# Local attention of a four-layer block: scores in 64-row halves, values three tiles behind, the next norm in its drain

## The chip, the cores and the metric

The kernel runs on one core of a Trainium2 chip. The metric is the device time of one launch in microseconds (us), the median of the runs shown. Engines are named as the profile names them: PE is the matrix engine (PEld its weight loads), DVE the vector engine, ACT the scalar engine, POOL the general-purpose engine, SP the engine that only issues DMAs. Each runs its own instructions strictly in order and waits on semaphores.

## The reference

Sixteen sequences of 1024 tokens with 256 features pass through four residual layers, each behind a layer norm without weights:

```
x = x + local_attention(layernorm(x), w_qkv, b_qkv)
x = x + ffn(layernorm(x), cn_*, gc_*, adaptive_range)
x = x + differential_attention(layernorm(x), Wq, Wk, Wv, Wo, ...)
x = x + ffn(layernorm(x), cn_*, gc_*, adaptive_range)
```

Local attention has 16 heads of 16 features. Every 32 neighbouring tokens form a group of their own, and attention is computed inside a group: `softmax(q k^T / 4) v` with 32x32 scores. Its output is reshaped without moving the heads back beside the features, so one "token" of the output holds one head's values of 16 tokens. The feed-forward layer (ffn) runs three cycles of a small gelu network (256 to 256 to 128 to 64 to 1) that sets one coupling factor per token, `out = out + coupling * twist(out)`, and adds to the factor a global one from the mean over all tokens of a sequence (`global_net`). Everything here is in float32, which PE works through in two passes: each float32 matmul stands in the trace as two records.

## The kernel before, in words

The 16 sequences are taken in 8 pairs, one turn of a hardware loop per pair. A turn is a chain of blocks, and each block ends when all engines have ended it: `local_attention`, `layernorm("n2")`, `ffn("f1")`, `layernorm("n3")`, `diff_attention`, `diff_output`, `layernorm("n4")`, `ffn("f2")`. The order of the instructions of each engine is written out by hand in each block.

**`local_attention`** takes a pair as 16 tiles of 128 tokens, t = 0 to 15, eight per sequence; a tile has four groups of 32 tokens. For each tile, with the line numbers of the kernel before:

- POOL copies the keys into `kx`, once for each head, with all rows but those of that head set to zero (L444). One instruction makes the 8 heads of one half c of the features: 8 times 128 columns. There are 4 buffers, so POOL can be two tiles ahead.
- PE, `scores` (L376): for each half c and each group k one matmul of 128 rows, weights the 32 queries of the group, moving 8 heads times 32 masked keys, to the 32 PSUM partitions of the group. The four groups stand in four column strips of the array. The scores of a tile fill one PSUM bank, and two banks alternate by t % 2, so a tile's scores wait for the `shift` of two tiles before.
- DVE: `maximum` (L469), `shift` (L473, subtracts the maximum and so frees the bank), and of the tile before `total` (L478), `inverse` (L482), and `turn` (L486 the division, L490 a transpose in 32x32 blocks).
- ACT: `exponentials` (L540), `keep` (L553, the values of tile t - 3 to `hT`) and `place` (L548, four copies that set the turned weights of tile t - 1 into a matrix with zeros around the groups). There are two such matrices.
- PE, `values` (L392): 16 matmuls, of tile t - 2 behind the scores of tile t.

Between these, PE projects the second sequence: four query and key pieces (L352) at t = 2 to 5 and four value pieces (L361) at t = 6 to 9 (and the first sequence's value pieces at t = 0 and 1), which ACT and DVE take out of PSUM (L534, L460). From t = 11 PE turns the first sequence's output into the reshaped order (`regroup`, L410), and DVE adds it to x (`residual`, L497) and takes the statistics for the next norm (L503). The second sequence's four `regroup` pieces come after the last tile, when nothing else is left.

**`layernorm("n2")`** then finishes the statistics of the second sequence (L244, L246, POOL's root L252), normalises 16 tiles of tokens on DVE (L271), turns them on PE (L258) and copies them back to SBUF as `hT` (ACT L304, DVE L277).

**`ffn("f1")`** begins with the mean over each sequence (DVE L1009) and its first layer: `layer1(n)` for chunk n of 512 tokens is four pieces of two matmuls each, two with `w1` and two with `w1t` (L697). The first matmuls of layer 2 are at L706; the global network is at L678 to L686.

Of the kernel before, what the change touches and what calls it, by code (L numbers as in the profile page):

```python
# [51 lines left out]
def build(nc, a, out, scratch, rows):  # L52
    B = a["x"].shape[0]
    PAIRS = B // PB
    with ExitStack() as ctx:
# [44 lines left out]
        hmask = sb("hmask", [P, LC])  # L100
# [152 lines left out]

        def norm_turned(pe, t, s_h, s_tp):
# [7 lines left out]
        def layernorm(tag, norm, ahead=None, stale=None):  # L262
# [3 lines left out]
            with nc.Block() as block:  # L266
                @block.vector
                def _(v):
                    def normalised(n):
                        for t in range(4 * n, 4 * n + 4):  # L270
                            v.tensor_scalar(h[:, t, :], x[:, t, :], mv[:, t, 0:1], rstd[:, t:t + 1],  # L271
                                            ALU.subtract, ALU.mult).then_inc(s_h, 1)

# [8 lines left out]
                    for n in range(N0, CH + 1):  # L282
                        if n < CH:
                            if n % NB == 0:
                                v.wait_ge(norm[2], n // NB + 1)
                            normalised(n)
# [20 lines left out]
        def local_attention(norm):  # L307
# [8 lines left out]
            kx = [hh[:, i * N:(i + 1) * N].rearrange("p (h n) -> p h n", h=LC) for i in range(4)]  # L316
# [23 lines left out]
            with nc.Block() as block:  # L340
                @block.tensor
                def _(pe):
# [23 lines left out]
                    def scores(t):  # L366
# [3 lines left out]
                        if t >= 2:  # L370
                            pe.wait_ge(s_sd, t - 1)
                        for c in range(C):
                            pe.wait_ge(s_kx, C * t + c + 1)
                            for k in range(BLK):
                                r = slice(k * LB, (k + 1) * LB)
                                mm = pe.matmul(ps[r, t % 2, c * 256:(c + 1) * 256],  # L376
                                               qkT[:, b, c, tb * P + k * LB:tb * P + (k + 1) * LB],
                                               kx[(C * t + c) % len(kx)][:, :, r],
                                               start=True, stop=True)
                            mm.then_inc(s_sc, 1)  # L380

                    def values(t):
# [1439 lines left out]
```

## Time and profile before

| | us |
|---|---|
| Median of 3 runs | 7971.05 (7957.34 to 7980.41) |
| The profiled execution, its own time | 7964.95 |
| Its span, first to last instruction | 7963.3 |

The profile puts PE at 7373.2 us busy (93% of the span), DVE at 6889.1 (87%), ACT at 6124.5 (77%) and POOL at 3628.6 (46%). Most of that is `diff_attention`. These are means over blocks with different limits; the blocks that the change touches are a small part of each turn and are read by themselves below. PE's clock has two levels, 1.2 and 2.4 GHz, and the granted clock is given as a share of the upper one: 0.963 over the span.

### The profile page before, as it was taken

To read this page: it belongs to the slowest core of one execution; us is meant where nothing else is said; L and a number is where in the kernel's file an instruction comes from. 1 tells how busy PE (TensorE), PEld (TensorE's weight loads), DVE (VectorE), ACT (ScalarE), POOL (GpSimd) and SP (SyncE) were. 2 spreads that over 40 slices of the span, in tenths; PEclk is the share of its full clock that TensorE was granted. 3 is DMA by queue.
4 is the path that set the end of the run, shared out by engine and by line. 5 is a ranking of instruction groups with operands and counts; after the bars stand their busy time and mean duration, and the time that the engine had idled before them with its cause. 6 is when DMAs were issued, how large, how long until landed. Compare 5 with 4: busy or idle time off the path is not lost. (4 is left out here: it accounts for less than half of the span.)

```text
span 7963.3 us, 182322 instructions
## 1 busy us (share of the span) xinstructions
PE 7373.2 (93%) x72640; PEld 3328.7 (42%) x72640; DVE 6889.1 (87%) x8962; ACT 6124.5 (77%) x11390; POOL 3628.6 (46%) x5187
## 2 busy tenths in 40 slices
PE   6899988999889998899988999889998999989999
PEld 4344443444434444344443444434444344443444
DVE  5899868997689976899769997699976999769997
ACT  3699756997569975699756997569975699756997
POOL 4366333663336623466234662346613466135661
PEclk9999999999999998999989999999999999999999
DMA  1122102120022100222002220021200222002210
GB/s 32 53 45 44 30 12 56 44 48 24 12 56 48 44 24 12 57 48 44 23 12 59 47 45 24 10 64 44 47 23 5 64 44 48 26 2 64 48 44 26
DMA packets 604400, 298.88 MB, mean 38 GB/s; under 512 B 487094, under 2 KB 528566, under 8 KB 603510
## 3 DMA queue, kind: packets, MB, share of 16 engines
q1 hardware_dynamic: 603516, 286.86, 14.8%
q8 instruction: 583, 9.55, 0.5%
q14 instruction: 301, 2.47, 0.1%
HBM read 123.84 MB, written 67.37 MB: 24 GB/s over the span
## 5 line engine op out<-in xcount | busy, mean ns | idle before, releaser
L1548 DVE TENSOR_REDUCE mall<-ps 128x1 f32<-128x1024 f32 x4096 | 4669.5, 1217 | 71.7 <-PE ps L1482 68.4
L1639 ACT ACTIVATE work<-ps 128x512 f32<-128x512 f32 x8192 | 4311.2, 603 | 164.0 <-PE ps L1498 39.9
L1514 PE MATMUL ps<-work,vbuf 128*32 128x256 f32 x32768 | 2624.3, 392 | 21.6
L1498 PE MATMUL ps<-qop,kop 51*128 51x256 bf16 x16384 | 2558.1, 273 | 10.6 <-ACT work L1639 8.8
L1482 PE MATMUL ps<-kop,qop 48*128 48x512 bf16 x8192 | 2535.4, 384 | 33.6 <-DMA kop<-scratch 18.8
L1498 PEld LDWEIGHTS ps<-qop,kop 51*128 51x128 bf16 x16384 | 1182.0, 94 | 1887.5 <-ACT work L1639 1596.1
L1514 PEld LDWEIGHTS ps<-work,vbuf 128*32 128x32 f32 x32768 | 661.8, 108 | 923.4 <-issue 591.1
L252 POOL TENSOR_TENSOR rstd<-rstd,nhalf 128x8 f32<-128x8 f32 x64 | 109.3, 1707 | 1501.9 <-DVE rstd L246 1501.9
L1573 POOL TENSOR_TENSOR mall<-mall 128x8 f32<-128x8 f32 x1024 | 212.9, 208 | 1254.9 <-DVE mall L1548 1214.8
L444 POOL TENSOR_TENSOR hh<-work,hmask 128x1024 f32<-128x1024 f32 x256 | 516.2, 2045 | 457.0 <-POOLq L1744 362.1
L1601 POOL TENSOR_TENSOR work<-work,none 128x16 f32<-128x16 f32 x224 | 650.4, 2904 | 18.1
L1482 PEld LDWEIGHTS ps<-kop,qop 48*128 48x128 bf16 x8192 | 538.5, 93 | 93.6 <-DVE mall L1548 58.7
L706 PE MATMUL ps<-work,w 128*128 128x512 f32 x768 | 401.4, 663 | 62.9 <-ACT work L843 62.9
L1598 POOL COPY work<-work 128x272 uint16<-128x272 uint16 x448 | 221.7, 495 | 478.5 <-DMA work<-work 464.4
L548 ACT COPY vbuf<-qop 32x512 f32<-32x512 f32 x512 | 315.2, 616 | 105.6 <-DVE qop L490 96.0
L1614 POOL TENSOR_TENSOR work<-work,nhalf 128x8 f32<-128x8 f32 x224 | 373.2, 1666 | 18.6
L258 PE MATMUL ps<-ident,hh 128*128 128x128 f32 x800 | 167.6, 390 | 161.6 <-DVE hh L271 83.2
L304 ACT COPY hh<-ps 128x512 f32<-128x512 f32 x80 | 46.9, 586 | 325.5 <-PE ps L258 325.5
L392 PE MATMUL ps<-vbuf,work 128*32 128x128 f32 x4096 | 159.7, 304 | 143.4 <-ACT vbuf L548 141.9
L1582 POOL COPY work<-hh 128x512 uint16<-128x512 uint16 x448 | 260.6, 611 | 42.5 <-ACT hh L1646 28.9
L706 PEld LDWEIGHTS ps<-work,w 128*128 128x128 f32 x768 | 153.6, 211 | 285.7 <-issue 165.9
L1646 ACT COPY hh<-ps 128x256 f32<-128x256 f32 x512 | 190.5, 372 | 90.7 <-PE ps L1514 90.7
(179 smaller groups left out, 8317.1 us busy)
## 6 DMA issues: line engine op xcount, KB each, us to landing
qop<-scratch SPq DMA_DIRECT2D x512, 64.0 KB
scratch<-work SPq DMA_DIRECT2D x32, 768.0 KB, 4.3
scratch<-hh SPq DMA_DIRECT2D x32, 768.0 KB, 3.8
kop<-scratch SPq DMA_DIRECT2D x256, 96.0 KB
vbuf<-in_x SPq DMA_DIRECT2D x9, 2048.0 KB, 8.4
qop<-scratch SPq DMA_DIRECT2D x512, 32.0 KB
kop<-scratch SPq DMA_DIRECT2D x256, 64.0 KB
qop<-mT SPq DMA_DIRECT2D x1024, 3.0 KB
```

Source lines behind the costliest of these rows:

```text
L444: pool.tensor_tensor(kx[i % len(kx)], qkT[:, b, 2 + c, tb * P:(tb + 1) * P][:, None, :].to_broadcast([P, LC, P]), hmask[:, :, None].to_bro ...
L548: act.copy(PT[t % 2][r, :, r], pr[t % 2][r]).then_inc(s_pa, 1)
L706: mm = pe.matmul(ps[:, 2 * n, :], w2[:, c, :], a1[n][:, c, :], start=c == 0, stop=c == C - 1)
L1482: pe.matmul(ps[:, b + n, :], qop[r:r + KQ, s, i, t * P:(t + 1) * P], kop[r:r + KQ, s, i, half(n)], start=True, stop=True).then_inc(s_ms, 1)
L1498: mm = pe.matmul(ps[:, bank, part * HQ:(part + 1) * HQ], kop[r:r + KM, s, i, (t + part) * P:(t + part + 1) * P], qop[r:r + KM, s, i, quart ...
L1514: mm = pe.matmul(ps[VW * i:VW * (i + 1), OB, kept], vp[:, b, t, (G * gl + i) // 2, :], prob[:, u % PS, i, cols], start=t == 0, stop=t == T ...
L1548: v.tensor_reduce(mall[:, m // CUT % 2, to, col:col + 1], ps[:, b:b + NB, :].rearrange("p b n -> p (b n)"), AX.X, ALU.max).then_inc(s_mr, 1)
L1582: pool.tensor_copy(plane16[u], src[:, :, u]).then_inc(s_pl, 1)
L1598: link(pool.tensor_copy(raw_halves[:, :, :, u], turned16[u].rearrange("p t (h w) -> p (t h) w", w=VW)[:, :, 0:LD + 1]))
L1601: link(pool.tensor_tensor(erz, y[:, :, LD], none[:, :], ALU.pow))
L1614: link(pool.tensor_tensor(err, esv, nhalf[:, 0:HV], ALU.pow))
L1639: act.activation(prob[:, u % PS, hl, :], ps[:, EB[slot % len(EB)], :], ACT.Exp, scale=scale).then_inc(s_ex, 1)
```

## The change

- **Scores.** The rows of a half c are cut in two: s = 0 is rows 0 to 63, the first four heads, s = 1 rows 64 to 127, the other four. The mask `hmask` has four columns instead of eight, so one POOL instruction writes 4 times 128 columns, in which each row half holds its own four heads. There are 8 buffers of half the size. A tile's scores are 16 matmuls of 64 rows and 128 moving columns instead of 8 of 128 rows and 256. Half s goes to bank s, so a tile uses both banks at once and its scores wait for the `shift` of the tile just before. DVE's `maximum` and `shift` read 256 columns of each of the two banks; the heads stand in another order, which `placed_at` undoes in `values`.
- **Values.** `values` runs three tiles behind the scores, not two.
- **The norm.** The block `layernorm("n2")` is gone. In `local_attention` DVE normalises the first sequence right behind the last `turn`, PE turns it (`first_turns`) ahead of the last `values`, and ACT and DVE copy it. In `ffn("f1")` PE does three of the four pieces of the first chunk, then turns the second sequence, then goes on; DVE's statistics, normalising and copies of the second sequence stand around the first mean.
- **Both ffn blocks.** The first step of the global network stands behind both `w1` pieces of chunk 1, not between them.
- A helper is renamed (`scaled`), and `normalised` becomes shared by the blocks.

```diff
-        hmask = sb("hmask", [P, LC])
+        hmask = sb("hmask", [P, LC // 2])
+        def normalised(v, n, s_h):
+            for t in range(4 * n, 4 * n + 4):
+                v.tensor_scalar(h[:, t, :], x[:, t, :], mv[:, t, 0:1], rstd[:, t:t + 1],
+                                ALU.subtract, ALU.mult).then_inc(s_h, 1)
...
-            kx = [hh[:, i * N:(i + 1) * N].rearrange("p (h n) -> p h n", h=LC) for i in range(4)]
+            kx = [hh[:, half(i)].rearrange("p (h n) -> p h n", h=LC // 2) for i in range(8)]
...
-                        if t >= 2:
-                            pe.wait_ge(s_sd, t - 1)
+                        if t >= 1:
+                            pe.wait_ge(s_sd, t)
                         for c in range(C):
                             pe.wait_ge(s_kx, C * t + c + 1)
-                            for k in range(BLK):
-                                r = slice(k * LB, (k + 1) * LB)
-                                mm = pe.matmul(ps[r, t % 2, c * 256:(c + 1) * 256],
-                                               qkT[:, b, c, tb * P + k * LB:tb * P + (k + 1) * LB],
-                                               kx[(C * t + c) % len(kx)][:, :, r],
-                                               start=True, stop=True)
+                            for s in range(2):
+                                heads = slice(s * P // 2, (s + 1) * P // 2)
+                                for k in range(BLK):
+                                    r = slice(k * LB, (k + 1) * LB)
+                                    mm = pe.matmul(ps[r, s, c * P:(c + 1) * P],
+                                                   qkT[heads, b, c, tb * P + k * LB:tb * P + (k + 1) * LB],
+                                                   kx[(C * t + c) % len(kx)][heads, :, r],
+                                                   start=True, stop=True)
                             mm.then_inc(s_sc, 1)
...
-                                                   vz[:, b, tb, i, :], PT[t % 2][:, i, :], start=e == 0, stop=e == 1,
+                                                   vz[:, b, tb, i, :], PT[t % 2][:, placed_at(i), :], start=e == 0, stop=e == 1,
...
+                    def first_turns():
+                        for t in range(T):
+                            pe.wait_ge(s_h, t + 1)
+                            for c, bank in enumerate((t // 4, VB + 2 + t // 4)):
+                                mm = pe.transpose(ps[:, bank, t % 4 * P:(t % 4 + 1) * P],
+                                                  h[:, t, c * P:(c + 1) * P], ident[:, :])
+                            mm.then_inc(s_tp, 1)
...
+                            if k >= 2:
+                                pe.wait_ge(s_ld, k - 1)
...
-                    for t in range(TT + 2):
+                    for t in range(TT + 3):
                         if t < TT:
                             scores(t)
-                        if t >= 2:
-                            values(t - 2)
+                        if t == TT + 3 - 1:
+                            first_turns()
+                        if t >= 3:
+                            values(t - 3)
...
-                        v.tensor_reduce(mx[:, t, :], scores_of(t), AX.X, ALU.max).then_inc(s_mx, 1)
+                        v.tensor_reduce(mx[:, t, :].rearrange("p (s h) -> p s h", s=2), scores_now, AX.X,
+                                        ALU.max).then_inc(s_mx, 1)
...
+                    v.wait_ge(norm[2], 1)
+                    for n in range(NB):
+                        normalised(v, n, s_h)
+                    for n in range(NB):
+                        v.wait_ge(s_tp, 4 * (n + 1))
+                        v.tensor_copy(hT[:, 0, 1, half(n)], ps[:, VB + 2 + n, :]).then_inc(s_ld, 1)
                     for k in range(4):
                         residual(1, k)
...
-                    layer1(0)
-                    layer1(1, ((0, 0),))
+                    if second_norm:
+                        layer1(0, ((0, 0), (0, 1), (1, 0)))
+                        for t in range(T, TT):
+                            norm_turned(pe, t, s_h0, s_tp0)
+                        layer1(0, ((1, 1),))
+                        pe.wait_ge(s_lc, CH)
+                        pe.wait_ge(s_ld, CH)
+                    else:
+                        layer1(0)
+                    layer1(1, ((0, 0), (0, 1)))
                     global_net(0)
-                    layer1(1, ((0, 1),))
...
-                    for b in range(PB):
+                    if second_norm:
+                        spread(v, norm0, 1)
+                    mean(0)
+                    if second_norm:
+                        v.wait_ge(norm0[2], 2)
+                        for n in range(NB, CH):
+                            normalised(v, n, s_h0)
+                        for n in range(NB, CH):
+                            second_keep(n)
+                    mean(1)
                     keep(0)
...
-            layernorm("n2", n2)
```

PE's order at t = 2 and 3 of `local_attention`, as a difference (L376 and L378 are the scores before and now, L392 and L399 the values, L352 the projection pieces; out and in are the buffers):

```order
-L376 MATMUL ps<-hh,work 32x256 x8
-L392 MATMUL ps<-vbuf,work 32x128 x16
+L378 MATMUL ps<-hh,work 32x128 x16
 L352 MATMUL ps<-hh,w_qkv 128x512 x4
-L376 MATMUL ps<-hh,work 32x256 x8
-L392 MATMUL ps<-vbuf,work 32x128 x16
+L378 MATMUL ps<-hh,work 32x128 x16
+L399 MATMUL ps<-vbuf,work 32x128 x16
 L352 MATMUL ps<-hh,w_qkv 128x512 x4
```

The first `values` have moved behind the scores of t = 3, and the scores are twice as many matmuls with half the columns.

PE's order from the last scores to the global network, before (L410 is `regroup`, L258 the norm's transposes, L697 the first layer of the ffn, L678 the global network's first step):

```order
L376 MATMUL ps<-hh,work 32x256 x8
L392 MATMUL ps<-vbuf,work 32x128 x48
L410 MATMUL ps<-ident,hh 64x64 x64
L340 UNCONDITIONAL_BRANCH
L294 UNCONDITIONAL_BRANCH
L258 MATMUL ps<-ident,hh 128x128 x32
L266 UNCONDITIONAL_BRANCH
L671 UNCONDITIONAL_BRANCH
L697 MATMUL ps<-hh,w 128x512 x4
L697 MATMUL ps<-hh,w1t 128x512 x4
L697 MATMUL ps<-hh,w 128x512 x2
L678 MATMUL ps<-work,g 128x2 x2
```

and the same place now (L408 are the `first_turns`, L263 the second sequence's transposes, L427 `regroup`, L732 the first layer, L713 the global network):

```order
L399 MATMUL ps<-vbuf,work 32x128 x48
L408 MATMUL ps<-ident,hh 128x128 x16
L399 MATMUL ps<-vbuf,work 32x128 x16
L427 MATMUL ps<-ident,hh 64x64 x64
L340 UNCONDITIONAL_BRANCH
L706 UNCONDITIONAL_BRANCH
L732 MATMUL ps<-hh,w 128x512 x4
L732 MATMUL ps<-hh,w1t 128x512 x2
L263 MATMUL ps<-ident,hh 128x128 x16
L732 MATMUL ps<-hh,w1t 128x512 x2
L732 MATMUL ps<-hh,w 128x512 x4
L713 MATMUL ps<-work,g 128x2 x2
```

One block with 32 transposes is gone; 16 of them stand ahead of the last tile's values, and 16 behind six matmuls of the first layer.

## Rows read from the trace of the kernel before

**Rows 1.** Windows of pairs 2 and 3: length, busy PE, PEld, DVE, ACT, POOL, clock.

```profile
1113.00:1137.00 24.00, 18.83 (x384) 13.94 (x376) 20.52 (x41) 16.44 (x31) 16.76 (x8) 1.00 0.01 2
2096.00:2123.00 27.00, 20.58 (x384) 15.30 (x376) 22.66 (x42) 16.32 (x30) 15.86 (x8) 0.87 0.01 2
```

**Rows 2.** Timeline, pair 2, tiles 8 to 10: start, us, engine, line, count, idle before.

```profile
1103.17 1.07 PE L376 MATMUL ps<-hh,work 128*32 128x256 f32 x16
1104.31 0.69 DVE L469 TENSOR_REDUCE work<-ps 128x16 f32<-128x512 f32 x1 [1.18 <-PE ps L376]
...
1107.15 2.54 ACT L548 COPY vbuf<-qop 32x512 f32<-32x512 f32 x4 [0.50 <-DVE qop L490]
...
1108.47 0.69 DVE L469 TENSOR_REDUCE work<-ps 128x16 f32<-128x512 f32 x1
...
1109.74 1.08 PE L392 MATMUL ps<-vbuf,work 128*32 128x128 f32 x32 [1.34 <-ACT vbuf L548]
...
1111.20 0.85 DVE L460 TENSOR_TENSOR work<-ps,b_v 128x128 f32<-128x128 f32 x4
...
1112.67 1.07 PE L376 MATMUL ps<-hh,work 128*32 128x256 f32 x16
```

**Rows 3.** Timeline of PE, pair 2, tiles 2, 3 and 6.

```profile
1069.85 1.07 PE L376 MATMUL ps<-hh,work 128*32 128x256 f32 x16
1072.14 1.08 PE L392 MATMUL ps<-vbuf,work 128*32 128x128 f32 x32 [1.22 <-ACT vbuf L548]
1073.15 3.70 PE L352 MATMUL ps<-hh,w_qkv 128*128 128x512 f32 x8
1076.78 1.07 PE L376 MATMUL ps<-hh,work 128*32 128x256 f32 x16
1077.67 1.06 PE L392 MATMUL ps<-vbuf,work 128*32 128x128 f32 x32
...
1093.60 1.07 PE L376 MATMUL ps<-hh,work 128*32 128x256 f32 x16
```

**Rows 4.** Timeline, pair 2, the first tile's keys and second half of scores.

```profile
1055.20 7.46 POOL L444 TENSOR_TENSOR hh<-work,hmask 128x1024 f32<-128x1024 f32 x4 [51.91 <-POOLq L1744]
...
1059.01 1.08 PE L376 MATMUL ps<-hh,work 128*32 128x256 f32 x8 [0.77 <-POOL hh L444]
```

**Rows 5.** Groups by line: out<-in, shapes, count, busy us, mean ns, idle.

```profile
L1602 POOL TENSOR_TENSOR work<-work 128x256 f32<-128x256 f32 x224 | 139.0, 620 | 17.6
L1163 DVE TENSOR_TENSOR work<-ps,cosT 128x1024 f32<-128x1024 f32 x64 | 77.7, 1215 | 2.7 <-PEq L266 2.4
```

**Rows 6.** Timeline of PE: sixteen transposes; two matmuls in two row halves.

```profile
1050.54 1.91 PE L789 MATMUL ps<-ident,hh 128*128 128x128 f32 x16
...
205.25 1.13 PE L722 MATMUL ps<-qop,w4r 64*128 64x512 f32 x4
```

**Rows 7.** Timeline, pair 2: the norm's first part, the ffn's start, layer 2.

```profile
1161.01 2.67 DVE L271 TENSOR_SCALAR hh<-x,mv,rstd 128x256 f32<-128x256 f32 x8
...
1168.99 4.48 DVE L1009 TENSOR_REDUCE work<-hh 128x2 f32<-128x2048 f32 x2 [0.30 <-PEq L266]
1168.99 3.67 PE L697 MATMUL ps<-hh,w 128*128 128x512 f32 x8 [1.03 <-PEq L266]
...
1179.81 1.88 PE L706 MATMUL ps<-work,w 128*128 128x512 f32 x4
```

**Rows 8.** Timeline of DVE, pair 2, the maxima of tiles 14 and 15.

```profile
1132.86 0.68 DVE L469 TENSOR_REDUCE work<-ps 128x16 f32<-128x512 f32 x1
...
1137.08 0.69 DVE L469 TENSOR_REDUCE work<-ps 128x16 f32<-128x512 f32 x1 [0.31 <-PE ps L376]
```

**Rows 9.** Timeline, pair 2: the last values and the last statistics.

```profile
1147.71 1.94 PE L392 MATMUL ps<-vbuf,work 128*32 128x128 f32 x32 [3.31 <-ACT vbuf L548]
...
1158.51 1.41 DVE L503 BATCH_NORM_STATS2 st<-x 128x6 f32<-128x256 f32 x4
```

**Rows 10.** Window over the norm and the ffn's start, pair 2; columns as in rows 1.

```profile
1160.00:1180.00 20.00, 17.23 (x61) 10.64 (x62) 14.26 (x33) 7.28 (x12) 1.89 (x1) 0.86 0.01 1
```

More of the change, by code:

```diff
@@ L304, in _, with local_attention @@
                         act.copy(hT[:, b, 0, cols], ps[:, 4 * b + n % NB, :])
-        def local_attention(norm):
+        def local_attention(norm, s_h, s_tp, s_lc, s_ld):
             qkT = work[:, 0:8 * N].rearrange("p (b m n) -> p b m n", b=PB, m=4)
@@ L564, in _ @@
                             qk_keep(1, t - 2)
+                    for n in range(NB):
+                        act.wait_ge(s_tp, 4 * (n + 1))
+                        act.copy(hT[:, 0, 0, half(n)], ps[:, n, :]).then_inc(s_lc, 1)
         def first_keys(pe, k, bank, s_qk):
@@ L619, in both, with ffn @@
             return shared[name]
-        def ffn(tag, norm, q=None, ahead=None, first_unit=None, following=None):
+        def ffn(tag, norm, q=None, ahead=None, first_unit=None, following=None, second_norm=None):
+            if second_norm:
+                norm0, s_h0, s_tp0, s_lc, s_ld = second_norm
             if following:
@@ L1006, in keep, with second_keep, mean @@
                             v.tensor_copy(V[n][:, m, :], ps[:, first_bank(n) + 2 + m, :]).then_inc(s_ev, 1)
-                    for b in range(PB):
-                        v.tensor_reduce(gm[:, :, b], hT[:, b, :, :], AX.X, ALU.add).then_inc(s_gm, 1)
+                    def second_keep(n):
+                        b, cols = chunk_of(n)
+                        v.wait_ge(s_tp0, 4 * (n + 1))
+                        v.tensor_copy(hT[:, b, 1, cols], ps[:, 4 * b + NB + n % NB, :]).then_inc(s_ld, 1)
+                    def mean(b):
+                        if second_norm:
+                            v.wait_ge(s_lc, NB * (b + 1))
+                            v.wait_ge(s_ld, NB * (b + 1))
+                        v.tensor_reduce(gm[:, :, b], hT[:, b, :, :], AX.X, ALU.add).then_inc(s_gm, 1)
+                    if second_norm:
+                        spread(v, norm0, 1)
+                    mean(0)
+                    if second_norm:
+                        v.wait_ge(norm0[2], 2)
+                        for n in range(NB, CH):
+                            normalised(v, n, s_h0)
+                        for n in range(NB, CH):
+                            second_keep(n)
+                    mean(1)
                     keep(0)
@@ L1728, in build @@
             n1, n2, n3, n4 = ([sem(f"n{i}_{n}") for n in ("mv", "var", "rs")] for i in (1, 2, 3, 4))
-            local_attention(n2)
-            layernorm("n2", n2)
+            n2_turn = [sem(f"n2_{n}") for n in ("h", "tp", "lc", "ld")]
+            local_attention(n2, *n2_turn)
             n3_ahead = [sem(f"n3_{n}") for n in ("h", "tp", "nb", "ln")]
             project = diff_project()
-            ffn("f1", n3, ahead=n3_ahead, first_unit=lambda pe: project[0](pe, first_unit=True))
+            ffn("f1", n3, ahead=n3_ahead, first_unit=lambda pe: project[0](pe, first_unit=True),
+                second_norm=[n2] + n2_turn)
             layernorm("n3", n3, ahead=n3_ahead)
@@ L1803 @@
         "ident": np.eye(P, dtype=np.float32),
-        "hmask": np.kron(np.eye(LC, dtype=np.float32), np.ones((LD, 1), np.float32)),
+        "hmask": np.tile(np.kron(np.eye(LC // 2, dtype=np.float32), np.ones((LD, 1), np.float32)), (2, 1)),
         "sign": column(np.ascontiguousarray(sign[:, 0])),
```

37 lines of the change are left out of this document (22 added, 15 removed).

## The prediction

> **What bounds the kernel now.** I read the windows over the touched blocks first, then the timeline of one pair, engine by engine, and last the groups by line for prices. Pair 2 is the template; what moves lies between a pair's first masked key and its first matmul of layer 2.
>
> Late in local attention no engine is full: in 24.0 us DVE is busy 20.5, PE 18.8, ACT 16.4 and POOL 16.8 [rows 1]. So a chain of waits sets the pace. Follow it [rows 2]: scores of tile 8 start at 1103.17, DVE's maximum at 1104.31, after 1.18 us of idle that PE ended; behind it `shift` and the `turn` of tile 7, then ACT's `place` of tile 7 at 1107.15 for 2.54 us, and PE, which had idled 1.34 us for it, starts the values of tile 7 at 1109.74; behind them in PE's queue stand a value piece and, at 1112.67, the scores of tile 10. One lap of this chain is 1112.67 - 1103.17 = 9.50 us for two tiles, 4.75 each.
>
> In tiles 2 to 5 PE itself is the bound [rows 3]: from the scores of tile 3 to those of tile 6 it takes 93.60 - 76.78 = 16.82 us, 5.61 a tile, of which scores, values and a projection piece (1.07, 1.06, 3.70) fill nearly all; at tile 2 it also idles 1.22 us for the first `place`.
>
> **The change, part by part, for pair 2.**
>
> *Masked keys.* POOL's instructions of 1024 columns take 7.46 / 4 = 1.87 us here, and the second half of the first scores waits for the second one (0.77 us after its own first half) until 1059.01, 3.81 us after the start [rows 4]. Half the columns: from one side half of 1.87 = 0.93, from the other the full price if a fixed cost ruled. A row with 256 columns of a like operation takes 0.62 [rows 5]; 512 lie between that and 1.87, near 1.1, which I take. Then the second half starts at 2 x 1.1 = 2.2, a gain of 1.6. After that POOL, with half the work, waits for nobody.
>
> *Scores.* Eight matmuls of 256 columns, four strips side by side, take from the start of the scores to the start of the values 77.67 - 76.78 = 0.89 us [rows 3]. Sixteen of 128 columns are the same number of columns; if the two row halves run side by side they take half, 0.44, otherwise 0.89. For the row halves the trace has one place: two matmuls of 512 columns on rows 0 to 63 and 64 to 127 take 1.13 us together [rows 6], while full-height ones of 512 columns take 3.67 / 4 = 0.92 each [rows 7]. So two row halves do share the time. Eight tiles at once (two halves, four strips) no row shows: between 0.44 and 0.89, and above that if the halves disturb each other. Next to it a change of tile shape: values to projection is 73.15 - 72.14 = 1.01 us where scores to values of one shape is 0.89 for as many columns, so a change of shape costs about 0.1 [rows 3]; now there is one more of them in each tile. I take 0.64 for the scores with their changes of shape, 1.00 for the values.
>
> The Trainium skill, "TensorEngine Tiling (Array Packing)", section Key Properties, speaks against this step: switching the tiling mode, not just the tile, drains the engine. The 0.1 us above is what this trace shows of such a drain. By the rule the scores would keep that cost; without any drain they would be 0.1 us shorter and the sum below 6 us larger.
>
> *Tiles 0 to 8.* Until scores 2 the way is as before, 1069.85 - 1059.01 = 10.84 us [rows 3, 4], less about 0.9 for a half and a whole set of scores: scores 2 start at 2.2 + 9.9 = 12.1 after the first key (14.65 before). Tile 2 has no values now: 0.64 + 3.63 (73.15 to 76.78 [rows 3]) = 4.27. Tiles 3 to 5: 0.64 + 1.00 + 3.63 = 5.27 each, 15.8. Scores 6 at 32.2 (before: 1093.60 - 1055.20 = 38.4). Tile 6: 0.64 and then 2.93 for values and value piece (1109.74 to 1112.67 [rows 2]) = 3.57, scores 7 at 35.8, their maximum at 36.5. From here PE needs less than DVE. A lap of DVE with a piece of values to take over is 1108.47 - 1104.31 = 4.16 us without idle time [rows 2], so the maximum of tile 8 stands at 40.7; before it stood at 49.1. Gain 8.4.
>
> *Tiles 8 to 15.* With values three behind, a lap of the old chain serves three tiles: 9.50 / 3 = 3.2 us each, under DVE's own 4.16. PE's wait for `place` goes, and what is late next is DVE. Its laps: tiles 8 to 10 at 4.16, 12.5 us; tile 11 without L460's 0.85 [rows 2], 3.3; tiles 12 to 14 with a residual, 1137.08 - 1132.86 - 0.31 idle = 3.91 each [rows 8], and once the statistics, 1.41 [rows 9], 13.1. Together 28.9, against 1137.08 - 1104.31 = 32.8 before. Gain 3.9. ACT (16.4 of 24.0 in [rows 1]) has the room. Scores now need the `shift` of the tile before, but DVE still has `turn` and `total` behind each `shift`, and PE's 0.64 lies beside these; without that cover it would cost some 0.5 us a tile. `keep` now waits in ACT's queue, ahead of `place`, for values issued behind the scores of its own tile: these end 0.64 + 1.00 after the scores start, before `shift` and `exponentials` of that tile are through, so it waits for nothing.
>
> *The drain.* After the last `turn`, DVE normalises eight tiles (2.67 us [rows 7]) beside ACT's `place` (2.54 [rows 2]); PE turns them as they come and so ends some 0.4 us later, and only then takes the last values, which before waited for `place` alone until 1147.71, after 3.31 us of idle [rows 9]. So 0.6 us lost. The copies lie under `regroup`.
>
> *The norm and the ffn.* Before, from the last statistics' end at 1158.51 + 1.41 = 1159.92 [rows 9] to layer 2 at 1179.81 [rows 7] it is 19.9 us: 9.1 of norm and block entries, 10.8 of PE's first layer. Now one block entry (estimated 0.3, as the part of 1161.01 - 1159.92 before the two short statistics operations), the same 10.8 of matmuls, and 16 transposes in PE's queue, 1.91 when their inputs are ready [rows 6]: 13.0. They are ready: DVE needs 1.1 for entry and statistics, 2.24 for a mean (4.48 / 2) and 2.67 for normalising [rows 7], 6.0, when PE has just done three of four pieces. The second mean, behind the copies, ends some 2 us before PE asks for it. But PE's clock is at half around here: 0.86 over 20 us [rows 10] is 5.6 us at the lower level, so far under transposes that waited for DVE anyway. Now dense matmuls stand there, and lose up to 2.8 us; I take 2.4. So 15.4, gain 4.5; bounds 2 and 6.9.
>
> The global network's first step moves behind one more piece in both ffn blocks. Its ACT answer comes while PE does layer 2 (1.88 us [rows 7]); I count nothing, and 0.5 us a block if that cover fails.
>
> *Sum.* The stretch from the first key at 1055.20 [rows 4] to layer 2 at 1179.81 [rows 7] is 124.6 us now, and loses 8.4 + 3.9 - 0.6 + 4.5 = 16.2 us in a pair, 130 in eight. Five pairs (3, 4, 5, 7, 8) lose 3 us more before, in the late tiles, with the clock at 0.87 over 27.0 us [rows 1]; PE has less to do there now, and will lie at half clock as readily, but off the path. I count half, 1.5 x 5 = 7. So 137 us off the profiled execution's 7964.95, 7828; the median lies 6 above it, 7834.
>
> **Rivals.**
>
> (a) Row halves don't overlap under four strips, so the scores with drains stay at 1.1. This costs 0.46 us in each of seven tiles up to tile 6, 3.2 a pair, 26 us in all: 7860. For it: no row has eight tiles at once. Against: the 1.13 us [rows 6].
>
> (b) The norm gives little: the clock stays low for the whole of the first layer, or DVE's new queue (mean, normalise, copies, mean) is late for the global network. Gain 1.5 instead of 4.5: 24 us, 7858. For it: the 0.86 [rows 10].
>
> (c) Values three behind don't do what they should: ACT's `keep` holds up `place` as before, and the two-tile chain remains. Then tiles 8 to 15 gain nothing, nor tiles 6 and 7 (1.2): 5.1 x 8 = 41, 7875. Against: the order of ends worked out above.
>
> (d) Slower: DVE's reads of scores now take 256 columns from each of two banks in a pattern of one more dimension. If that halves their rate, `maximum` and `shift` cost 0.69 us more each, 1.4 in each of 16 laps, 177 us in all: 7834 + 177 = 8011. It decides from 137 / 128 = 1.07 us a lap. Against: DVE reads 1024 columns over two banks in 1.21 us [rows 5], no more a column than L469's 0.69 for 512.
>
> (e) More than forecast: the clock stays up, in the late tiles and at the ffn's start: 15 more in the first, 2.4 x 8 = 19 in the second, 7800.
>
> **How the numbers follow.** Forecast 0.55 (7815 to 7855), (a) 0.12, (b) 0.12, (c) 0.08, (d) 0.04, (e) 0.09. The range from 7800 to 7885 takes in all but (d) and the mixtures of (a) to (c), which may reach 7910. A difference under 0.3% (24 us) is about what a measurement of this kernel can't tell from none. Faster 0.94: all but (d) and a small share of mixtures with unknown waits; same 0.02; slower 0.04.
>
> **What would show it.** PE's groups of scores with a start of values 0.55 to 0.7 us behind; POOL's rows near 1.1; the wait of values for `place` gone before tile 13, and DVE's maxima of tiles 8 to 15 without idle time, 4.16 and 3.9 us apart; 93 us from the first key to the last statistics (104.7 before), and 15 to layer 2. Wrong would be values waiting for `place`, maxima waiting for PE after tile 8, reads of DVE over 0.8 us, or 18 us or more from the last statistics to layer 2.

## The result: 1.4% faster, inside the range, with two errors that nearly hide each other

| | us |
|---|---|
| Before, median of 4 runs | 7966.18 (7957.34 to 7980.41) |
| After, median of 4 runs | 7855.36 (7850.25 to 7871.98) |
| Ratio, 95% interval | 0.9863 (0.9841 to 0.9884) |
| After, the profiled execution and its span | 7853.81, 7852.2 |

Forecast were 7834 and 7800 to 7885. So the change gave 111 us between the profiled executions, where 137 were worked out.

**The late tiles.** The window over pair 2, in the columns of [rows 1]:

```profile
1088.00:1112.00 24.00, 17.97 (x480) 15.13 (x480) 23.72 (x49) 19.84 (x37) 2.25 (x3) 0.90 0.01 3
```

DVE is now busy 23.72 us of 24.0 (20.52 in [rows 1]): it sets the pace. The timeline of tiles 8 to 10, with the starts of [rows 2]:

```profile
1078.40 0.67 PE L378 MATMUL ps<-hh,work 64*32 64x128 f32 x32
...
1078.83 2.54 ACT L578 COPY vbuf<-qop 32x512 f32<-32x512 f32 x4
...
1079.00 1.08 PE L399 MATMUL ps<-vbuf,work 128*32 128x128 f32 x32
...
1080.08 0.68 DVE L491 TENSOR_REDUCE work<-ps 128x16 f32<-128x512 f32 x1
...
1084.11 0.68 DVE L491 TENSOR_REDUCE work<-ps 128x16 f32<-128x512 f32 x1
```

The values start 0.60 us behind the scores (1079.00 - 1078.40) and wait for nothing; the maxima of tiles 8 and 9 are 4.03 us apart and have no idle time in brackets. Later tiles, with a residual in place of the value piece ([rows 8]):

```profile
1104.50 0.68 DVE L491 TENSOR_REDUCE work<-ps 128x16 f32<-128x512 f32 x1
...
1108.34 0.68 DVE L491 TENSOR_REDUCE work<-ps 128x16 f32<-128x512 f32 x1
```

These are 3.84 us apart. Of PE's waits (engine, line, waited for: us in total over all turns, times, longest), this is the one of the values for `place`, before and now. What is left of it now, two waits a turn, stands behind the last scores:

```profile
PE ps L392 <- ACT vbuf L548: 141.9, 79, 3.4
PE ps L399 <- ACT vbuf L578: 37.3, 16, 2.8
```

**The first tiles.** PE in pair 2, with the first keys ([rows 3, 4]):

```profile
1037.12 8.03 POOL L463 TENSOR_TENSOR hh<-work,hmask 128x512 f32<-128x512 f32 x8 [49.63 <-POOLq L1815]
...
1040.51 0.64 PE L378 MATMUL ps<-hh,work 64*32 64x128 f32 x5 [0.64 <-issue]
1041.08 6.13 PE L361 MATMUL ps<-w_qkv,hh 128*128 128x256 f32 x16
...
1047.74 3.72 PE L361 MATMUL ps<-w_qkv,hh 128*128 128x256 f32 x16
...
1051.39 0.67 PE L378 MATMUL ps<-hh,work 64*32 64x128 f32 x32
...
1071.33 0.67 PE L378 MATMUL ps<-hh,work 64*32 64x128 f32 x32
```

Scores 2 start 14.27 us after the first key, not 12.1. The eight projections of the first value pieces begin 3.96 us after the first key, where the forecast implies some 2.7 (2.2 and half a set of scores); 0.64 us of the difference is a stop for which the profile shows no wait. Then they take 6.13 us, and 3.72 the second time. But before they did not run at full clock either; here is their row, and the windows over the first 14 us of both traces (before, then after; columns as in [rows 1]):

```profile
1060.02 5.25 PE L361 MATMUL ps<-w_qkv,hh 128*128 128x256 f32 x16
...
1055.00:1069.00 14.00, 11.08 (x61) 7.33 (x62) 5.92 (x16) 2.54 (x3) 13.80 (x8) 0.76 0.02 5
...
1037.12:1051.00 13.88, 11.61 (x95) 8.55 (x96) 6.02 (x15) 2.47 (x3) 13.88 (x12) 0.75 0.02 5
```

The granted clock is the same, 0.76 and 0.75: in both traces one stretch of 6.8 us stands at half clock, from 1.1 us after the first key before and from 2.0 us now. PE is busy for 6.1 us of it now, and was for 5.2 before. From scores 2 to scores 6 it is 19.94 us (20.1 forecast).

**The norm and the ffn's start** ([rows 7, 9]):

```profile
1130.68 1.41 DVE L527 BATCH_NORM_STATS2 st<-x 128x6 f32<-128x256 f32 x4
...
1132.42 6.51 PE L732 MATMUL ps<-hh,w 128*128 128x512 f32 x8 [2.51 <-PEq L340]
...
1138.77 1.88 PE L732 MATMUL ps<-hh,w1t 128*128 128x512 f32 x4
...
1140.49 1.91 PE L263 MATMUL ps<-ident,hh 128*128 128x128 f32 x16
...
1143.95 3.60 PE L732 MATMUL ps<-hh,w 128*128 128x512 f32 x8
...
1147.75 1.96 PE L741 MATMUL ps<-work,w 128*128 128x512 f32 x4
```

From the last statistics' end (1132.09) to layer 2 it is 15.66 us. The transposes take the 1.91 us of a run without waits; the first four matmuls (eight records) take 6.51 us at half clock, where the last four take 3.60.

**Where the rest of the gain went.** I cut every turn of both traces, one profiled execution each, at the same marks (first masked key, maxima 8 and 15, end of the last statistics, first matmul of layer 2, first and last maximum of the differential attention, next turn) and summed over eight turns; us:

| kernel | to max 8 | 8 to 15 | to last stats | to layer 2 | to diff. attention | its maxima | rest |
|---|---|---|---|---|---|---|---|
| before | 396.6 | 277.0 | 182.5 | 159.1 | 996.6 | 4692.4 | 1191.8 |
| after | 339.4 | 226.1 | 188.4 | 122.3 | 1001.8 | 4723.1 | 1184.4 |

The first four columns lose 139 us, two more than forecast. But 31 come back in the maxima of the differential attention, which the change does not touch: 586.0 to 587.3 us a turn before, after 590.1, 593.8, 590.9, 586.0, 593.8, 591.0, 585.9, 591.6. (The two columns beside them, 5 us more and 7 less, nearly cancel; no run sorts them.) The windows over the first 37.4 us of it in turns 2 and 4 of the kernel after, for the maxima's reductions alone (length, DVE busy and count, clock, DMA):

```profile
1273.50:1310.90 37.40, 27.57 (x24) 0.52 0.37 123
3221.70:3259.10 37.40, 34.16 (x30) 0.91 0.39 126
```

In turn 2 PE is at half clock, and 24 reductions stand where turn 4 has 30; six at 1.25 us are 7.5 of the 7.8 us that turn 2 lost. What PE did at the place in turn 2, after and (last row) before:

```profile
1262.69 7.07 PE L1204 MATMUL ps<-wv,hh 128*128 128x256 f32 x32
1272.90 0.59 PE L1552 MATMUL ps<-kop,qop 48*128 48x512 bf16 x2 [3.14 <-DMA kop<-scratch]
1273.41 1.13 PE L1204 MATMUL ps<-wv,hh 128*128 128x256 f32 x4
1274.48 1.36 PE L1552 MATMUL ps<-kop,qop 48*128 48x512 bf16 x4
1275.76 2.07 PE L1204 MATMUL ps<-wv,hh 128*128 128x256 f32 x4
...
1302.43 0.59 PE L1482 MATMUL ps<-kop,qop 48*128 48x512 bf16 x2 [2.19 <-DMA kop<-scratch]
```

PE now waits 3.14 us for the keys' DMA (2.19 us before), and the value products behind it go from 1.13 to 2.07 us. (The matmuls with the keys are in bf16 and stand as one record each, float32 ones as two, transposes as one.) That this wait is the cause was a theory at this point; the experiments test it.

### The profile page after: what moved, and what is told of

It reads as the page before. It is cut to its first block and busy times, and to the rows that moved or that the text cites. A ratio compares the mean times of both kernels' runs of the same rounds, so it can differ in the third digit from the quotient of the medians.

```text
span 7852.2 us, 186378 instructions
## 1 busy us (share of the span) xinstructions
PE 7368.5 (94%) x74688; PEld 3337.0 (42%) x74688; DVE 6883.9 (88%) x8962; ACT 6121.9 (78%) x11390; POOL 3382.1 (43%) x5187
## 5 line engine op out<-in xcount | busy, mean ns | idle before, releaser
L463 POOL TENSOR_TENSOR hh<-work,hmask 128x512 f32<-128x512 f32 x256 | 264.8, 1063 | 525.6 <-POOLq L1815 357.6
L1652 POOL COPY work<-hh 128x512 uint16<-128x512 uint16 x448 | 261.7, 614 | 42.6 <-ACT hh L1716 28.9
L732 PE MATMUL ps<-hh,w 128*128 128x512 f32 x512 | 252.7, 640 | 28.3 <-PEq L340 20.1
L1682 POOL TENSOR_TENSOR work<-work 128x64 f32<-128x64 f32 (+3 forms) x896 | 222.8, 249 | 70.1
L263 PE MATMUL ps<-ident,hh 128*128 128x128 f32 x672 | 129.2, 359 | 128.9 <-DVE hh L256 53.8
```

Of the source, the lines that this page charges most:

```text
L463: pool.tensor_tensor(kx[i % len(kx)], qkT[:, b, 2 + c, tb * P:(tb + 1) * P][:, None, :].to_broadcast([P, LC // 2, P]), hmask[:, :, None].t ...
L732: mm = pe.matmul(ps[:, first_bank(n) + 2 * k + m, :], w[:, c, m * P:(m + 1) * P], hT[:, b, c, cols], start=c == 0, stop=c == C - 1)
L1652: pool.tensor_copy(plane16[u], src[:, :, u]).then_inc(s_pl, 1)
```

## The experiments

The table of marks, continued for each kernel that was run. The columns come from one profiled execution; the ratio is that of the medians of 4 to 12 timed runs to those of the kernel before on the same chip. Where the text says how many us an edit takes off, it is this ratio's share of the kernel before.

| kernel | to max 8 | 8 to 15 | to last stats | to layer 2 | to diff. attention | its maxima | rest | ratio (95%) |
|---|---|---|---|---|---|---|---|---|
| scores_only | 396.7 | 269.0 | 181.7 | 159.1 | 997.3 | 4694.8 | 1189.8 | 0.9982 (0.9973 to 0.9991) |
| values_only | 362.2 | 240.2 | 182.4 | 159.1 | 989.0 | 4700.5 | 1187.4 | 0.9906 (0.9893 to 0.9920) |
| norm_only | 407.5 | 274.2 | 185.5 | 110.7 | 995.0 | 4714.7 | 1184.5 | 0.9981 (0.9970 to 0.9992) |
| after_fill | 338.5 | 225.8 | 187.1 | 119.0 | 999.3 | 4692.0 | 1184.2 | 0.9817 (0.9805 to 0.9830) |
| before_fill | 396.8 | 283.7 | 183.4 | 159.1 | 987.8 | 4692.3 | 1189.8 | 1.0002 (0.9992 to 1.0012) |
| no_values_fill | 393.1 | 269.3 | 189.2 | 118.6 | 998.8 | 4690.6 | 1186.3 | 0.9937 (0.9920 to 0.9954) |
| no_scores_fill | 363.9 | 240.2 | 188.1 | 118.3 | 996.4 | 4695.9 | 1183.8 | 0.9862 (0.9846 to 0.9879) |
| no_norm_fill | 338.2 | 226.0 | 182.3 | 159.1 | 997.0 | 4689.0 | 1189.3 | 0.9860 (0.9843 to 0.9876) |
| fill_drain | 338.2 | 225.9 | 187.2 | 103.8 | 994.5 | 4688.9 | 1187.0 | 0.9789 (0.9775 to 0.9802) |
| fill_all | 339.5 | 225.9 | 189.5 | 103.8 | 1000.6 | 4692.2 | 1201.7 | 0.9818 (0.9804 to 0.9831) |

**Scores alone.** The kernel before with the changes to `kx`, `hmask`, `scores`, `maximum`, `shift` and `placed_at`; the loop of PE stays:

```diff
-                                               qkT[:, b, c, tb * P + k * LB:tb * P + (k + 1) * LB],
-                                               kx[(C * t + c) % len(kx)][:, :, r],
...
+                                                   qkT[heads, b, c, tb * P + k * LB:tb * P + (k + 1) * LB],
+                                                   kx[(C * t + c) % len(kx)][heads, :, r],
...
                         if t >= 2:
                             values(t - 2)
```

> The kernel before with the scores' edit alone: 64-row halves, masked keys of 512 columns, both score banks for one tile, values still two behind, the layernorm where it was. Theory: POOL's masked keys set the first nine tiles, so the maximum of tile 8 comes 41 to 44 us after the first masked key (before 49.1), while the values' wait for the place of their tile stays and the maxima from tile 8 to tile 15 still take 30 to 33 us; the last statistics to layer 2 stay near 20 us; 60 to 85 us off the whole, 7880 to 7905 us. Rival: with both banks held by one tile the scores of a tile wait for the shift before them and stand behind values that wait for the place, so that tiles 8 to 15 become slower than before (34 us or more) and eat the gain: 7920 us or more.

Measured: 7955.72, 14 us off (7 to 22 by the interval). The theory misses, in the time and in both stages; the rival's time (7920 or more) holds, but its stage does not. Tiles 8 to 15 take 33.6 us a turn, between the theory's 30 to 33 and the rival's 34, and less than the 34.6 of the kernel before. The maximum of tile 8 comes at 49.6 us in the mean, as before (theory 41 to 44). PE in tiles 2 to 4 of pair 2 shows why:

```profile
1063.91 0.67 PE L378 MATMUL ps<-hh,work 64*32 64x128 f32 x32
1067.23 1.41 PE L399 MATMUL ps<-vbuf,work 128*32 128x128 f32 x32 [2.65 <-ACT vbuf L560]
1068.57 5.01 PE L352 MATMUL ps<-hh,w_qkv 128*128 128x512 f32 x8
1073.51 0.67 PE L378 MATMUL ps<-hh,work 64*32 64x128 f32 x32
1074.11 1.08 PE L399 MATMUL ps<-vbuf,work 128*32 128x128 f32 x32
1075.12 3.70 PE L352 MATMUL ps<-hh,w_qkv 128*128 128x512 f32 x8
1078.75 0.67 PE L378 MATMUL ps<-hh,work 64*32 64x128 f32 x32
1080.07 1.08 PE L399 MATMUL ps<-vbuf,work 128*32 128x128 f32 x32 [0.65 <-ACT vbuf L560]
```

The time that the scores save is spent in front of the values, waiting for `place`: 2.65 us at tile 2 (1.22 in [rows 3]), then 0.65 at every other tile. That wait grows to 173.5 us over the kernel, from 141.9. So the two-tile chain over `place` already holds the first tiles as soon as PE gets a little faster. The clock adds to it: the projection piece behind this wait takes 5.01 us, the next one 3.70. In six turns of eight the trace has 3.4 us at half clock there, and the maximum of tile 8 comes at 49.4 to 50.4 us; in the other two it comes at 47.7 and 47.8. That the wait is what lowers the clock there was not tested.

**Values alone.** One loop bound and two indices in the kernel before:

```diff
-                    for t in range(TT + 2):
+                    for t in range(TT + 3):
...
-                        if t >= 2:
-                            values(t - 2)
+                        if t >= 3:
+                            values(t - 3)
```

> The kernel before with the values three tiles behind the scores, and nothing else. Theory: the first tiles are bound by the masked keys, so the maximum of tile 8 stays at 49 us; from tile 8 on, the values no longer wait for the place and the maxima 8 to 15 take 29 to 31 us instead of 32.8, so 15 to 30 us off the whole, 7936 to 7951 us. Rival: the wait for the place only moves to the keys or the shift, and the time is that of before (7961 to 7971 us).

Measured: 7895.93, 75 us off (64 to 85), 2.5 to 5 times the theory. Tiles 8 to 15 take 30.03 us, as forecast; the miss is in the first tiles, where the maximum of tile 8 comes at 45.3 us instead of staying at 49. PE there has no wait at all:

```profile
1062.28 1.07 PE L376 MATMUL ps<-hh,work 128*32 128x256 f32 x16
1063.17 1.06 PE L392 MATMUL ps<-vbuf,work 128*32 128x128 f32 x32
1064.16 3.70 PE L352 MATMUL ps<-hh,w_qkv 128*128 128x512 f32 x8
1067.79 1.07 PE L376 MATMUL ps<-hh,work 128*32 128x256 f32 x16
```

5.51 us a tile, all of it PE's own work, so the masked keys of full width do not bound it, as I had written into this expectation. But before it was 5.61 [rows 3], so the gain of 3.9 us in pair 2 lies elsewhere: from scores 2 to scores 3 it is 4.64 us for 6.93, since tile 2 has no values and no wait for `place`, and tiles 6 and 7 take 3.80 us each, where the two took 9.6 us before with the wait in the second.

**Norm alone.** `first_turns`, `second_norm` and what belongs to them in the kernel before, the place of the global network's first step included; PE's loop ends at `TT + 2`:

```diff
+                        if t == TT + 2 - 1:
+                            first_turns()
...
-            layernorm("n2", n2)
```

> The kernel before with the first layernorm's work in the drain of the local attention and in the feed-forward network, scores and values as before. Theory: the last statistics to the first layer-2 product shrink from 20 to 15.5 us in each of 8 turns, 35 to 42 us off: 7924 to 7931 us. Rival: layer 1 then starts at half clock and gives half of it back: 7945 us or more.

Measured: 7949.72, 15 us off (6 to 24). By the time the rival is right, by the stage neither: from the last statistics to layer 2 it is 13.8 us a turn, 48 us less in all and more than forecast, since in five turns of eight the clock stays up (12.8 us there, 15.4 to 15.6 in the others). What is missing stands in other columns: 22 us in the differential attention, and 11 in the first tiles, where the maximum of tile 8 comes at 52.6 to 53.1 us in four turns and at 49.1 in the others. Before, only the first turn had 52.8. These turns, and no others of the two traces, have a second stretch of 3.4 us at half clock, which begins 19 to 20 us after the first key. An edit that is worth 48 us where it acts is worth 24 in the sum of this profiled execution, and 15 by the medians.

**The wait filled.** In the changed kernel, behind the value projection ahead of the differential attention, six matmuls whose result nobody reads (the products, below):

```diff
                 for t in range(T):
                     project_values(pe, t)
+                pe.wait_ge(s_ve, 1)
+                for _ in range(6):
+                    pe.matmul(ps[:, 0, 0:D], hT[:, 0, 0, 0:P], wv[:, 0, :], start=True, stop=True)
                 pe.wait_ge(s_ve, T // 2)
```

> The changed kernel with six more products of 256 fp32 columns on TensorE (their result is never read) between the last value projection ahead of the differential attention's first scores and those scores, where TensorE waits 2.5 to 3.2 us for the keys' DMA. Theory: the 28 us by which the change came out smaller than forecast are TensorE at half clock at the start of the untouched differential attention, and the clock falls after this wait: with the wait filled the clock stays at 1.00 there, the first to the last maximum's reduction take 586 us in all 8 turns (now 586 to 593.8), and the time is 7822 to 7835 us. Rival: the clock falls because of the light products behind the wait, or the lost time is not the clock's: then the same 590 to 594 us in five of eight turns, and 7850 to 7860 us.

Measured: 7824.69, ratio 0.9817 against 0.9863. The maxima take 586.0 to 586.8 us in all eight turns, as the theory said. PE at the place, and then the window that answers to the two above, again for the reductions:

```profile
1265.32 2.81 PE L1199 MATMUL ps<-wv,hh 128*128 128x256 f32 x12
1268.07 0.60 PE L1555 MATMUL ps<-kop,qop 48*128 48x512 bf16 x2
1268.60 1.13 PE L1207 MATMUL ps<-wv,hh 128*128 128x256 f32 x4
```

```profile
1268.70:1306.10 37.40, 34.31 (x30) 0.91 0.39 127
```

The products end as the keys arrive, the value products behind stay at 1.13 us, and clock and count are the 0.91 and 30 of an undisturbed turn. So PE's idle wait is where the clock is lost: filled, it costs nothing, and the light matmuls behind it (48 rows, bf16) are no cause by themselves.

The Trainium skill, "TensorE: Matmul & The Clock Gate", section "Why this matters for your kernels", advises against idle gaps of TensorE (PE here) between bursts of matmuls. This trace agrees in direction; but in turn 4 of the changed kernel PE waited 2.66 us at the same place, and the products behind it show the full clock:

```profile
3221.10 0.59 PE L1552 MATMUL ps<-kop,qop 48*128 48x512 bf16 x2 [2.66 <-DMA kop<-scratch]
3221.62 1.13 PE L1204 MATMUL ps<-wv,hh 128*128 128x256 f32 x4
```

In turn 6 it waited 2.65 us and was then at half clock for 17.1 us. Which of such waits costs the clock, the runs don't say.

**The same products in the kernel before.**

> The kernel before with the same six products in TensorE's wait ahead of the differential attention's first scores. Theory: in the kernel before the clock stayed at 1.00 there in five turns of eight and was at half for 3.4 us in three, so there is next to nothing to win: the maxima's reductions take 586.0 to 586.8 us in every turn and the time is 7958 to 7968 us. Rival: the products help by themselves, whatever the kernel: 20 us or more off, below 7947 us.

Measured: 7962.57, ratio 1.0002 (0.9992 to 1.0012); maxima 585.9 to 587.2 us. The rival falls: the products win nothing where the clock was up. They give back what the changed kernel lost, and are no gain of their own. (The theory's 586.0 to 586.8 us a turn was too narrow, and the late tiles now lose some 3 us to the clock in seven turns, where five did so before: so far do the clock's falls move when the only edit is in another block.)

**One edit taken back at a time**, with the products, so that the clock there cannot blur the count:

```diff
# no_values_fill
-                    for t in range(TT + 3):
+                    for t in range(TT + 2):
# no_scores_fill
-                            for s in range(2):
-                                heads = slice(s * P // 2, (s + 1) * P // 2)
# no_norm_fill
+            layernorm("n2", n2)
```

> The changed kernel with the six products ahead of the differential attention, but with the values two tiles behind the scores again. Theory: the two-tile chain over the place of the values comes back and holds both halves of the local attention, as in the run with the scores' edit alone: the maximum of tile 8 at 48 to 50 us, tiles 8 to 15 in 33.5 us, 92 to 100 us more than with the values three behind: 7915 to 7925 us. Rival: the edits add up, and the values are worth the 71 us that they gave alone: 7896 us.

Measured: 7913.82, 1 us under the theory's bound; 1.20% of the time above the run with all edits, 96 us.

> The changed kernel with the six products ahead of the differential attention, but with the scores and masked keys as before (full height, 1024 columns, alternating banks). Theory: with the chain over the place gone, TensorE and the keys bound the first tiles, so the scores' edit is worth what the run with the values alone lacks: the maximum of tile 8 at 45 us instead of 42.3, tiles 8 to 15 in 30.0 instead of 28.2 us, about 33 us in all: 7852 to 7863 us. Rival: the scores' edit is worth the 11 us that it gave alone: 7836 us.

Measured: 7854.07; 0.45%, 36 us. The maximum of tile 8 comes at 45.5 us in the mean, tiles 8 to 15 take 30.03, as the theory said.

> The changed kernel with the six products ahead of the differential attention, but with the first layernorm as a block of its own again. Theory: from the last statistics to layer 2 it is 19.9 us again instead of 12.8 to 15.6, and the drain gets some 0.6 us a turn back: 33 to 40 us more, 7857 to 7865 us. Rival: the norm's edit is worth the 17.5 us that it gave alone: 7842 us.

Measured: 7851.31; 0.43%, 34 us by the ratios, which are what compares runs of two chips (the median itself is 6 us under the bound that I gave). By these sums each edit is worth more on top of the others than alone (96, 36 and 34 against 75, 14 and 15), but each difference is only about as large as its interval, some 20 us, and the runs alone had no products. The columns tell two cases apart. To the maximum of tile 15 the scores are worth 40 us on top and 8 alone, the values 98 and 71: this is the two edits' own doing. The values take away the wait that stands behind the scores, and without that wait PE's own work is what the scores shorten. From the last statistics to layer 2 the norm is worth 40 us on top and 48 alone, so it does not gain from the others; alone it lost 22 us in the differential attention, where the other runs had the products.

**More of the clock.** Five products behind the last `regroup`, before the ffn:

```diff
                     for k in range(4):
                         regroup(1, k)
+                    for _ in range(5):
+                        pe.matmul(ps[:, 2, 0:D], w_qkv[:, 0, 0:P], w_qkv[:, 1, 0:D], start=True, stop=True)
```

> The changed kernel with the six products ahead of the differential attention and five more (256 fp32 columns, never read) behind the last regroup of the local attention, where TensorE idles 2.5 us before the first layer of the feed-forward network. Theory: the idle time lets the clock fall, and the first layer's eight matmuls take 6.4 us instead of 3.6; with it filled the clock stays up, the last statistics to layer 2 take 12.8 us in all turns (now 15.4 to 15.6 in six of eight), and 15 to 20 us go: ratio to the kernel before 0.979 to 0.980, near 7805 us. Rival: the clock falls because of the many small matmuls of the regroup ahead of the idle time; the products then run at half clock, take 4 us and delay the first layer: 15.5 us or more still, no gain or a loss of up to 10 us.

Measured: 7796.25, ratio 0.9789 (0.9775 to 0.9802), 22 us below the run with six products. It is the fastest kernel of this study. The last statistics to layer 2 take 12.97 or 12.98 us in every turn:

```profile
1115.00 7.48 PE L427 MATMUL ps<-ident,hh 128*64 128x64 f32 x128 [0.50 <-ACT hh L585]
1122.41 2.43 PE L450 MATMUL ps<-w_qkv 128*128 128x256 f32 x10
1125.15 3.67 PE L734 MATMUL ps<-hh,w 128*128 128x512 f32 x8 [0.31 <-PEq L340]
```

The products run at full clock (1.00 over their 2.43 us), so the `regroup` had not lost it; of the 2.51 us that PE waited for the block 0.31 are left, and the first four matmuls of the layer take 3.67 us for 6.51.

And besides, six products at the end of the second ffn and two ahead of the first scores:

> As the run with the products at both places, and besides with six products behind the last transposes of the second feed-forward block and two ahead of the first scores, where TensorE idles 3.9 us between two turns. Theory: the first scores and the sixteen products of the first value pieces now run at half clock (5.5 us instead of 3.7 for the first eight); at full clock the maximum of tile 8 comes at 40.7 us in all turns instead of 42.3, 10 to 14 us less over eight turns than without: ratio 0.977 to 0.9785, near 7793 us. Rival: the products are late for the first keys and cost what the clock gives, or the clock falls anyway: the ratio of the run without them, within 0.001.

Measured: 7822.73, ratio 0.9818. The theory misses. The rival is right that nothing is gained, but it allowed 0.001 against the run without them, and the loss is 0.0029, 23 us. PE at the change of turns:

```profile
1029.46 2.75 PE L840 MATMUL ps<-w_qkv 128*128 128x256 f32 x12
1034.39 1.12 PE L432 MATMUL ps<-w_qkv 128*128 128x256 f32 x4 [2.18 <-PEq L1825]
...
1036.34 0.42 PE L378 MATMUL ps<-hh,work 64*32 64x128 f32 x7 [0.44 <-POOL hh L467]
1038.32 0.66 PE L378 MATMUL ps<-hh,work 64*32 64x128 f32 x9 [1.57 <-issue]
1038.90 5.98 PE L361 MATMUL ps<-w_qkv,hh 128*128 128x256 f32 x16
```

The next turn begins some 2 us after the last engine has ended, in this run and in the one without these products, and now that engine is PE, held up by the products: the rest of the turn grows by 15 us over eight turns, half of what the profiled execution lost. (Most of the other half stands ahead of the differential attention and in its maxima, and was not followed up.) Nothing of any engine stands in these 2 us, and behind them the clock falls all the same, in the middle of the first scores: the value piece takes 5.98 us.

## Why the prediction was right, and where it was not

- **The stretch that was worked out** lost 139 us against 137. To the maximum of tile 8 it was 57 (8 x 8.4 = 67 forecast), 8 to 15 it was 51 (8 x 3.9 + 7 = 38), the drain cost 6 (5), the norm gave 37 (36). Two terms are off by 10 and 13 us and cancel; that the sum of this stretch came out within 2 us is luck.
- **Masked keys**: 1.06 us a half instruction on average (1.1 taken). **Scores**: 0.60 us with the change of shape (0.64 taken), so rival (a) falls. Behind that row: the Trainium skill, "TensorEngine Tiling (Array Packing)", section "Key Properties", says that different tiles work in parallel; sixteen matmuls in eight tiles in 0.60 us, where eight of twice the columns in four took 0.89, agree. How much of the 0.60 us a change of shape costs, no row separates.
- **Tiles 0 to 8** missed by the start alone: scores 2 came at 12.06 to 15.14 us instead of 12.1, at 14.27 in pair 2. That the way to scores 2 is "as before" was the wrong step: the first value pieces took 6.13 us where they had taken 5.25, and began 3.96 us after the first key and not 2.7. PE is busy for more of the stretch at half clock (6.1 of 6.8 us for 5.2), and part of the late start is the stop of 0.64 us, which stays unexplained. From there on the sum held.
- **Tiles 8 to 15** took 28.26 us in every turn (28.9 forecast). The five turns that lost 3 us at half clock before lose nothing now (15 us in the table, 7 counted). The clock did not stay up, as (e) had it: every turn still has 3.4 us at half clock there, and as the sum said they are off the path. (In (e) these 15 us stand in full, though the sum had counted 7 of them already.)
- **The norm**: 15.5 to 15.8 us in seven turns, 15.4 forecast, with the half clock that was charged; 12.8 in the one turn where it stayed up. Rival (b) falls. **DVE's reads** of two banks: 0.68 and 0.65 us, as before; rival (d) falls.
- **Rival (c)** did not occur, but the run that comes nearest to it, values two behind again, costs 96 us and not 41. Of the 98 in the columns 55 lie before the maximum of tile 8, where (c) had counted 10. What failed there is "In tiles 2 to 5 PE itself is the bound", carried over to a kernel with faster scores and values two behind: the chain over `place` lay just under PE there, and the 1.22 us in [rows 3] said so.
- **The term that was missing** is about the size of the miss: 31 us in the differential attention, where the time came out 21 us above the forecast. I summed the stretch that the change touches and took the rest as given. The six products, which do nothing but fill that wait, give back 0.46% of the time, 37 us, and 31 in the column of the maxima.
- **The range** held for another reason than the one it was drawn for. Its upper part was there for (a) to (c), and 7855 us is close to what (a) and (b) alone give, 7860 and 7858; by the time alone one of them would look right, and the rows above rule out both.

Not settled is why PE's wait for the keys' DMA is 2.5 to 3.2 us after and 2.0 to 2.8 before in an untouched block, and which of these waits costs the clock: turns 2 and 5 after lost it for 37.5 us, 1, 3, 6 and 8 for 17.1, and 4 and 7 not at all. That it is no matter of one edit the runs do show: without the products the same loss stands in turn 4 of the scores alone (592.6 us), in 6 and 8 of the values alone (591.4), and in four turns of the norm alone (590.1 to 594.7).

## What to carry to other kernels

When a chain is lengthened from two tiles to three, look where it lies just under the bound that is seen: a faster engine there gains little until the chain is gone, so price edits in both orders. After any change of time in one block, read the granted clock at the next places where PE waits for a DMA or a block's end; a few products that keep it busy through such a wait can be worth as much as an edit, where nothing waits for their end.

## What the runs showed of the hardware that was not expected

- Five matmuls (ten records, 2.43 us) whose result nobody reads, ahead of the ffn, gave back 2.4 to 2.7 us in each turn where the clock had fallen: the four matmuls behind took 3.67 us for 6.51.
- Half clock for 17 to 37 us cost 4 to 8 us where light matmuls (48 rows, bf16) feed reductions. The 3.4 us in the late tiles of every turn after cost nothing: DVE is busy 23.72 of 24.0 us, and its lap there takes the 4.03 us of the laps at full clock.
- At the start of a turn PE's first scores stop without any wait that the profile shows: in seven turns of eight after, for 0.21 to 1.24 us, and for 1.57 us in pair 2 with all products. Each stop lies in a stretch at half clock; the one turn without a stop is the one where the clock falls only behind these scores. What that is stays open.
